# Two late steps for the first norm's halves and the second norm's routing in a fused attention and expert kernel

## Chip, cores and metric

One core of one Trainium2 chip. The metric is the device time of one execution in microseconds, median over runs; the kernel before has 318.69 us, median of 3 runs (318.09 to 318.78).

## What is computed

The input is 4 images of 128 channels and 32 x 32 positions, so 1024 tokens of 128 features each. Cut to what matters here:

```python
x = x + nin(softmax(q k^T / sqrt(128)) v)          # group norm, then one attention over 1024 positions
t = to_tokens(x)                                   # (4, 1024, 128)
u = ln(t)                                          # the first norm
k = softmax(u Wk, over tokens); ctx = k^T (u Wv)   # linear attention, 4 heads of 32
t = t + (u Wq) ctx Wout + b_out
w = ln(t)                                          # the second norm
probs = softmax(w router^T); top 2 of 8 experts, weights rescaled to sum 1
t = t + w + sum_e combine[:, e] * (gelu(w W1[e] + b1[e]) W2[e] + b2[e])
```

## The kernel before

The program is written out by hand for each engine: PE (matrix engine), ACT, DVE, POOL and the DMA queue SP. Each works through its own list in order and waits on semaphores. The first part handles the 4 images as batches: full attention of batch b, beside it the linear attention of batch b-1 and the routing of batch b-2. Then comes the **expert stage**, the subject here. It runs over 4 batches of 16 steps (2 halves of 512 tokens times 8 experts), 64 steps in all, numbered 0 to 63. In each step:

- PE: `hidden` forms the scores of one expert for one half of 512 tokens with `product3` (three matmuls of 512 columns, L1449 to L1451, from the high and low parts of `wT` and `w1`); it waits for the gelu of two steps earlier, since there are two score banks. Then `outward` forms the second product of the expert five steps earlier (`LAG` = 5) into the bank `ring`, with three matmuls again, or, for the steps in `WHOLE` (4, 6, 16, 18, 19, 20, 22, 28, 29, 30, 33, 34, 35, 37, 38, 40), with one in full float32 (L1805).
- ACT: `gelu` (L867, scores to `gel`), then `high` (L878), the high part of the weighed values of the step before; `WHOLE` steps have none.
- DVE: `weigh` (L1335, `gel` times the combine weights of that expert, which SP has spread over all partitions in one of four slots: `k_both`, `prob`, two halves of `pT_hi`), then `lower` (L1344, the low part of the step before). After five steps of a new half, `result` (L1356) adds the output bank, in PSUM, to the residual `z_in`.

The linear attention of the last batch and the routing of the last two are not done yet when the stage begins. They are put between the steps. `gathered` makes a table from step number to actions, and `between_steps` runs, on each engine, the actions of that number after that step's own work. The numbers stand in two tables, `TAIL_AT` (first half of the stage) and `END_AT` (last batch's routing). The units the prediction speaks of:

- `u0`, `u1`: PE turns (transposes, L1464) four 128x128 tiles of the first norm's result `u` each, and ACT copies them to `uT` (L741). POOL makes `u` in `first_norm` by eight instructions of 128x128 (`layer_norm`, L589), and signals after the fourth and the eighth. Its inputs are the mean and deviation that DVE hands it.
- `kT`: the keys (PE L1591 from `uT`), whose maximum DVE takes (`key_maximum`, L1112); ACT forms their exp, PE turns that back as `p0`, `p1`.
- `w0`, `w1`: the same for the second norm's result `w_n` (POOL L589): PE turns a half, ACT copies its high part (L745), DVE makes its low part (L1028).
- `lg`: the router's logits (PE L1640, L1641); ACT copies them (L765); `lT`: PE turns them (L1649). `rA`, `rB`, `rC`: DVE's top-2 and combine weights, some twenty short instructions from L1175 to L1212; `exp`: ACT's exponential for them (L771), with a table load before and after it. `z`: PE turns the residual that POOL made by `normed_residual` (L600), ACT copies it. `c`: PE turns the combine weights, DVE copies them (L1155), SP stores them and loads them back spread over the partitions (`load_shares`, L438).

The order of POOL's work is `w_n` of batch 2, `u` of batch 3 (`first_norm`), the residual L600 of batch 2, later `add_bout`, and then `w_n` and L600 of batch 3. The units' PSUM banks are dealt out in the order of the list `TAIL_UNITS` by `place_of`: the units after `OT1` take banks 0, 1 of `ring` and 2, 3 of `scores` in turn.

```python
def between_steps(steps, m, s):
    for step in steps.get(m * 2 * E + s, ()) if steps else ():
        step()
def turn_u(place, lb, n):
    pe.wait_ge(u_made, lb * HALVES + n + 1)
    turn(place, f"u{n}", tiles_of(u, n))
```

Of the kernel before, what the change touches and what calls it, by code (L numbers as in the profile page):

```python
# [47 lines left out]
LINEAR = dict(u=["u0", "u1"], kT=["kT0", "kT1"], p=["p0", "p1"])  # L48
ROUTING = dict(o=["o0", "o1"], w=["w0", "w1"], lg=["lg0", "lg1"], z=["z0", "z1"], c=["c0", "c1"])
# [9 lines left out]
                  OT1=1, v0=0, v1=1, T0a=2, T0b=3, T1a=0, T1b=1, xT0=2, xT1=3, w0=0, w1=1, T2a=2, T2b=3,  # L59
# [3 lines left out]

TAIL_FIRST = 2
TAIL_UNITS = (ATTENTION["T"][6] + ["ctx"] + ATTENTION["T"][7] + ["m2", "m3", "PV1"] + ROUTING["o"]
              + ["OT1"] + ROUTING["w"] + LINEAR["u"] + ROUTING["lg"] + ["lT"] + LINEAR["kT"]
              + ROUTING["z"] + LINEAR["p"] + ROUTING["c"] + ["g"])

END_UNITS = (["ctx", "m2", "m3"] + ROUTING["o"] + ROUTING["w"] + ROUTING["lg"] + ["lT"]
             + ROUTING["z"] + ROUTING["c"])  # L70


TAIL_AT = dict(m3=0, PV=1, o=2, st=2, OT=5, OTst=6, w0=9, w1=9, lg=12, u0=14, u1=14, lT=16, rA=17, kT=20, exp=20, rB=20, ks=23, z=21, p=21, rC=20, g=23, c=23)
END_AT = dict(ctx=24, m2=25, m3=27, o=29, st=29, w0=36, w1=36, lg=37, lT=38, rA=38, exp=38, rB=38, rC=38, z=41, c=41)

PIECES = 8
LAG, HELD, RING, PARTED = 5, 8, 6, 2
# [55 lines left out]
def conv_attention_moe(nc, x, gn_scale, gn_bias, wq, bq, wk, bk, wv, bv, wp, bp,  # L133
# [28 lines left out]
    with ctx:  # L162
# [145 lines left out]
        def gathered(*steps):  # L308

            found = {}  # L310
            for at, step in steps:
                found.setdefault(at, []).append(step)
            return found
# [370 lines left out]
        def _(act):  # L684
# [43 lines left out]
            def take_o(place, g):  # L728
                wait_filled(act, place, f"PV{g}")
                act.activation(o_s[:, :], ps(place, f"PV{g}"), ACT.Copy).then_inc(drained[place.bank(f"PV{g}")], 1)  # L730
# [8 lines left out]
            def turn_u(place, n):  # L739
                wait_filled(act, place, f"u{n}")  # L740
                act.activation(half(uT, n), ps(place, f"u{n}"), ACT.Copy).then_inc(drained[place.bank(f"u{n}")], 1)  # L741

            def turn_normed(place, kind, n, hi, made):
                wait_filled(act, place, f"{kind}{n}")
                act.activation(hi[n], ps(place, f"{kind}{n}"), ACT.Copy).then_inc(made, 1)  # L745

            def key_softmax(place, lb):

                act.wait_ge(k_max, lb + 1)
                for n in range(HALVES):  # L750
                    act.activation(half(p1, n), ps(place, f"kT{n}"), ACT.Exp, bias=kst[:, 2:3],
                                   accum_out=kst[:, 4 + n:5 + n]).then_inc(drained[place.bank(f"kT{n}")], 1)
# [8 lines left out]
            def take_logits(place):  # L761
                for n in range(HALVES):
                    unit = f"lg{n}"
                    wait_filled(act, place, unit)
                    act.activation(half(lgT, n), ps(place, unit)[0:2 * E, :], ACT.Copy  # L765
                                   ).then_inc(drained[place.bank(unit)], 1)

            def route_exp(place, lb):

                wait_drained(act, place, "lT")  # L770
                act.activation(rt[:, 1, :, :], rt[:, 0, :, :], ACT.Exp).then_inc(r_exp, 1)  # L771
# [9 lines left out]
            def w_halves(lb):  # L781
                return [wT_hi[:, bass.ds(lb * T + n * BANK, BANK)] for n in range(HALVES)]
# [97 lines left out]
            def experts(m, between):  # L880
# [10 lines left out]
            linear_and_routing = gathered(  # L891
                (TAIL_AT["PV"] + 3, lambda: take_o(TAIL, 1)),
                *((TAIL_AT["w" + str(n)], lambda n=n: turn_normed(TAIL, "w", n, w_halves(lc), w_hi_made)) for n in range(2)),
                *((TAIL_AT["u" + str(n)], lambda n=n: turn_u(TAIL, n)) for n in range(2)),
                (TAIL_AT["lg"], lambda: take_logits(TAIL)),
                (TAIL_AT["exp"], lambda: route_exp(TAIL, lc)),
                (TAIL_AT["exp"], lambda: key_softmax(TAIL, la)),
                (TAIL_AT["z"], lambda: turn_z(TAIL, lc, zT_late)),
                (TAIL_AT["p"], lambda: turn_keys(TAIL)),
                *((END_AT["w" + str(n)], lambda n=n: turn_normed(END, "w", n, w_halves(la), w_hi_made)) for n in range(2)),  # L900
                (END_AT["lg"], lambda: take_logits(END)),
                (END_AT["exp"], lambda: route_exp(END, la)),
                (END_AT["z"], lambda: turn_z(END, la, zT_late)),
            )
# [8 lines left out]
        def _(dve):  # L913
# [212 lines left out]
            def take_g(place):  # L1126
                take(place, "g", gT_s[:, :])
                wait_drained(dve, place, "g")
                dve.sem_inc(g_made, 1)
# [243 lines left out]
            def experts(m, between):  # L1373
# [37 lines left out]
                (TAIL_AT["g"], lambda: take_g(TAIL)),  # L1411
                (END_AT["ctx"], lambda: take_ctx(END)),
                (END_AT["m2"], lambda: take(END, "m2", m2T_s[:, :])),
                (END_AT["m3"], lambda: take(END, "m3", m3[:, :])),
# [472 lines left out]
```

## Time and profile before

| | before |
|---|---|
| median of 3 runs | 318.69 us (318.09 to 318.78) |
| profiled execution | span 315.6 us, first to last instruction (the page gives no other time for it) |
| PE busy | 297.7 us, 94% |
| DVE busy | 254.9 us, 81% |
| ACT busy | 200.8 us, 64% |
| POOL busy | 154.1 us, 49% |
| granted TensorE clock | 1.000 of full speed, mean |
| chain that ended last | PE 66%, DVE 13%, POOL 9%, ACT 7%, issue 3% |
| expert stage | from about 189 us on |

Busy time is the union of an engine's instructions. A matmul's end is modelled, so that the starts of matmuls, not their lengths, tell the pace of PE. The idle time of an engine is put down to what released it.

### The profile page before, as it was taken

The page shows a single profiled execution, that of the slowest core. Times are in us where ns is not written, and L with a number is a line of the kernel's source. Part 1 is how long each engine was busy: PE and PEld are TensorE (multiplying, and loading weights), DVE is VectorE, ACT ScalarE, POOL GpSimd, SP SyncE. Part 2 cuts the span into 40 slices and gives each one's busy share as a digit, 9 for nine tenths or more (in the row PEclk, how much of TensorE's full clock was granted, in tenths as well). Part 3 has the DMA queues.
Part 4 walks back from the last instruction along what each step waited for, and adds up shares of the span by engine and source line. Part 5 has one row for each costly group of instructions (what it writes and reads, how often), then busy time and mean ns, then how long its engine had stood idle before and what let it go on. Part 6 is the DMA issues. An engine that isn't in the chain of part 4 may idle for free.

```text
span 315.6 us, 5504 instructions
## 1 busy us (share of the span) xinstructions
PE 297.7 (94%) x1584; PEld 238.3 (76%) x1584; DVE 254.9 (81%) x635; ACT 200.8 (64%) x352; POOL 154.1 (49%) x358
## 2 busy tenths in 40 slices
PE   5898989989999999999999999998799998999996
PEld 4776768866878887878887797875677786668885
DVE  4599686587587799987698887999598896999996
ACT  3447474566771587663279577468578645888882
POOL 2899593059941985980784300599604049200000
PEclk9999999999999999999999999999999999999999
DMA  5902000010000021000000118395321783229801
GB/s 136 330 12 70 0 1 2 0 66 2 1 3 0 0 69 39 30 12 0 0 1 0 66 38 271 117 391 212 124 86 67 279 300 119 75 87 375 295 7 66
DMA packets 12904, 29.61 MB, mean 94 GB/s; under 512 B 2208, under 2 KB 6224, under 8 KB 10960
## 3 DMA queue, kind: packets, MB, share of 16 engines
q1 hardware_dynamic: 12448, 28.87, 26.3%
q10 hardware_dynamic: 432, 0.46, 0.4%
q8 instruction: 10, 0.16, 0.2%
q14 instruction: 14, 0.11, 0.1%
HBM read 24.73 MB, written 4.59 MB: 93 GB/s over the span
## 4 chain that ended last, share of the span: by engine, by line
PE 66%; DVE 13%; POOL 9%; ACT 7%; issue 3%; DMA 1%; DVEq 0%; POOLq 0%
PE ring L1464 11%; PE ring L1449 7%; PE ring L1451 7%; PE ring L1450 7%; PE scores L1449 6%; PE scores L1451 6%; PE scores L1450 6%; POOL w_n L589 3%; PE ring L1805 3%; POOL u L589 3%; ACT pT_hi L726 3%; ACT prob L720 2%; PE ring L1604 2%; DVE pT_lo L1059 2%; PE ring L1591 2%
## 5 line engine op out<-in xcount | busy, mean ns | idle before, releaser
L867 ACT ACTIVATE gel<-scores,b_c 128x512 f32<-128x512 f32 x64 | 43.9, 689 | 19.5 <-PE scores L1451 18.0
L1059 DVE TENSOR_TENSOR pT_lo<-ring,pT_hi 128x512 fp32r<-128x512 f32 x64 | 40.5, 681 | 9.8 <-ACT pT_hi L726 9.4
L720 ACT ACTIVATE prob<-prob,row_max 128x1024 f32<-128x1024 f32 x32 | 36.8, 1149 | 14.2 <-DVE prob L1052 14.2
L580 POOL TENSOR_SCALAR rstd<-lmv 128x4 f32<-128x4 f32 x16 | 4.3, 266 | 82.3 <-DVE lmv L1094 81.1
L1052 DVE TENSOR_SCALAR_CACHE_REDUCE prob<-scores 128x1024 f32<-128x1024 f32 x32 | 38.6, 1214 | 3.3 <-PE scores L1451 3.3
L726 ACT ACTIVATE pT_hi<-ring 128x512 fp32r<-128x512 f32 x64 | 34.6, 599 | 10.3 <-PE ring L1464 9.9
L1464 PE MATMUL ring<-ident,prob 128*128 128x128 f32 x256 | 33.7, 275 | 3.6 <-ACT prob L720 1.9
L1464 PEld LDWEIGHTS ring<-ident,prob 128*128 128x128 f32 x256 | 28.7, 140 | 8.5 <-ACT prob L720 3.7
L1449 PE MATMUL scores<-wT_hi,w_hi 128*128 128x512 f32 x64 | 29.3, 458 | 0.0
L1449 PE MATMUL scores<-k_both,q_hi 128*128 128x512 f32 x64 | 26.9, 421 | 1.9 <-DVE k_both L1037 1.3
L1449 PE MATMUL ring<-pT_hi,v_hi 128*128 128x512 f32 x64 | 26.5, 415 | 0.8 <-DVE pT_lo L1059 0.8
L1451 PE MATMUL scores<-k_both,q_lo 128*128 128x512 f32 x64 | 25.2, 393 | 0.0
L1451 PE MATMUL scores<-wT_hi,w_lo 128*128 128x512 f32 x64 | 25.1, 392 | 0.0
L1450 PE MATMUL scores<-wT_lo,w_hi 128*128 128x512 f32 x64 | 25.1, 392 | 0.0
L1450 PE MATMUL scores<-k_both,q_hi 128*128 128x512 f32 x64 | 25.1, 392 | 0.0
L1451 PE MATMUL ring<-pT_hi,v_lo 128*128 128x512 f32 x64 | 25.0, 391 | 0.0
L1450 PE MATMUL ring<-pT_lo,v_hi 128*128 128x512 f32 x64 | 25.0, 390 | 0.0
L611 POOL TENSOR_TENSOR t<-t,bout_row 128x128 f32<-128x128 f32 x32 | 14.0, 476 | 18.4 <-PE scores L1464 10.8
L730 ACT ACTIVATE o_s<-ring 128x512 f32<-128x512 f32 x8 | 4.8, 598 | 24.7 <-PE ring L1451 24.7
L589 POOL TENSOR_SCALAR u<-t,rstd 128x128 f32<-128x128 f32 x32 | 18.8, 608 | 0.9 <-POOL rstd L584 0.9
L589 POOL TENSOR_SCALAR w_n<-t,rstd 128x128 f32<-128x128 f32 x32 | 17.2, 555 | 0.9 <-POOL rstd L584 0.9
L584 POOL TENSOR_TENSOR rstd<-rstd,minus_half 128x4 f32<-128x4 f32 x16 | 16.6, 1040 | 0.0
(300 smaller groups left out, 780.9 us busy)
## 6 DMA issues: line engine op xcount, KB each, us to landing
pT_hi<-scratch_s SPq DMA_DIRECT2D x8, 1024.0 KB, 7.6
prob<-scratch_s SPq DMA_DIRECT2D x4, 1024.0 KB, 7.2
k_both<-scratch_s SPq DMA_DIRECT2D x3, 1024.0 KB, 5.8
z_in<-scratch_z SPq DMA_DIRECT2D x8, 256.0 KB, 2.9
out_dram<-out_s SPq DMA_DIRECT2D x7, 256.0 KB, 2.2
xb<-in_x_dram SPq DMA_DIRECT2D x3, 512.0 KB, 3.3
scratch_z<-out_s SPq DMA_DIRECT2D x2, 512.0 KB, 2.8
k_both<-scratch_s SPq DMA_DIRECT2D x4, 256.0 KB, 4.2
```

The lines of the kernel that those rows point to most:

```text
L584: pool.tensor_tensor(std[:, tiles], std[:, tiles], minus_half[:, tiles], ALU.pow).then_inc(ln_small[n], 1)
L589: last = pool.tensor_scalar(dst[:, j, :], src[:, j, :], neg[:, j:j + 1], std[:, j:j + 1], ALU.add, ALU.mult)
L611: last = pool.tensor_tensor(tiles_piece(t2, n), tiles_piece(t1, n), tiles_piece(bout_b, n), ALU.add)
L720: act.activation(prob[:, i % 2, :], prob[:, i % 2, :], ACT.Exp, bias=row_max[:, i:i + 1], scale=-1.0, accum_out=row_sum[:, 0, i:i + 1]).th ...
L726: act.activation(tile_group(pT_hi, n, i), as_tiles(ps(place, unit)), ACT.Copy).then_inc(p_hi_made, 1)
L867: act.activation(half(gel, s % 2), scores[:, s % 2, :], ACT.Gelu, bias=b1_c[:, s % E:s % E + 1]).then_inc(e_gelu, 1)
L1052: dve.tensor_scalar(prob[:, i % 2, :], scores[:, 2 * (i % 2):2 * (i % 2) + 2, :].rearrange("p a t -> p (a t)"), -SCALE, None, ALU.mult, AL ...
L1059: dve.tensor_tensor(tile_group(pT_lo, n, i), as_tiles(ps(place, unit)), tile_group(pT_hi, n, i).bitcast(FP32), ALU.subtract).then_inc(drai ...
L1449: pe.matmul(dst, lh, rh, start=start, stop=False)
L1450: pe.matmul(dst, lh, rl, start=False, stop=False)
L1451: return pe.matmul(dst, ll, rh, start=False, stop=stop)
L1464: last = pe.transpose(dst[0:t.shape[-1], j * step:j * step + rows], t, ident[0:rows, 0:rows])
```

## The change

Two tables of step numbers and one list change. In the expert stage, `u0` moves from step 14 to 15 and `u1` from 14 to 17, on PE and ACT. In the last batch's routing `w0` stays at step 36, and `w1` (PE, ACT and DVE), the logits, their turn, the whole of DVE's routing, ACT's exp, `z` and `c` each come one step later. The list `TAIL_UNITS` is put in the same order, by which the banks of `lg`, `u` and `lT` are dealt anew. No instruction is added or removed; POOL's and SP's order stays.

```diff
 TAIL_UNITS = (ATTENTION["T"][6] + ["ctx"] + ATTENTION["T"][7] + ["m2", "m3", "PV1"] + ROUTING["o"]
-              + ["OT1"] + ROUTING["w"] + LINEAR["u"] + ROUTING["lg"] + ["lT"] + LINEAR["kT"]
+              + ["OT1"] + ROUTING["w"] + ROUTING["lg"] + ["u0", "lT", "u1"] + LINEAR["kT"]
               + ROUTING["z"] + LINEAR["p"] + ROUTING["c"] + ["g"])
...
-TAIL_AT = dict(m3=0, PV=1, o=2, st=2, OT=5, OTst=6, w0=9, w1=9, lg=12, u0=14, u1=14, lT=16, rA=17, kT=20, exp=20, rB=20, ks=23, z=21, p=21, rC=20, g=23, c=23)
-END_AT = dict(ctx=24, m2=25, m3=27, o=29, st=29, w0=36, w1=36, lg=37, lT=38, rA=38, exp=38, rB=38, rC=38, z=41, c=41)
+TAIL_AT = dict(m3=0, PV=1, o=2, st=2, OT=5, OTst=6, w0=9, w1=9, lg=12, u0=15, u1=17, lT=16, rA=17, kT=20, exp=20, rB=20, ks=23, z=21, p=21, rC=20, g=23, c=23)
+END_AT = dict(ctx=24, m2=25, m3=27, o=29, st=29, w0=36, w1=37, lg=38, lT=39, rA=39, exp=39, rB=39, rC=39, z=42, c=42)
```

On ACT, from the gelu of step 14 on (L867 gelu, L878 high part, L741 copy of a half of `u`; `pT_lo` and `h_hi` hold high parts here). Before:

```order
L867 ACTIVATE gel<-scores,b_c 128x512
L878 ACTIVATE pT_lo<-hs 128x512
L741 ACTIVATE uT<-scores 128x512
L741 ACTIVATE uT<-ring 128x512
L867 ACTIVATE gel<-scores,b_c 128x512
L878 ACTIVATE pT_lo<-h_f 128x512
L867 ACTIVATE gel<-scores,b_c 128x512
L878 ACTIVATE pT_lo<-h_f 128x512
L867 ACTIVATE gel<-scores,b_c 128x512 x2
```

Now:

```order
L867 ACTIVATE gel<-scores,b_c 128x512
L878 ACTIVATE pT_lo<-hs 128x512
L867 ACTIVATE gel<-scores,b_c 128x512
L878 ACTIVATE pT_lo<-h_f 128x512
L741 ACTIVATE uT<-ring 128x512
L867 ACTIVATE gel<-scores,b_c 128x512
L878 ACTIVATE pT_lo<-h_f 128x512
L867 ACTIVATE gel<-scores,b_c 128x512
L741 ACTIVATE uT<-scores 128x512
L867 ACTIVATE gel<-scores,b_c 128x512
L878 ACTIVATE h_hi<-hw 128x512
```

Both copies of `u` stood between the high part of step 13 and the gelu of step 15; the first now stands behind the high part of step 14, the second behind the gelu of step 17.

On PE, behind the hidden product of step 14 (L1464 on `u` is a half's turn). Before:

```order
L1449 MATMUL ring<-h_hi,w_hi 128x512
L1450 MATMUL ring<-h_lo,w_hi 128x512
L1451 MATMUL ring<-h_hi,w_lo 128x512
L1464 MATMUL scores<-ident,u 128x128 x4
L1464 MATMUL ring<-ident,u 128x128 x4
L1449 MATMUL scores<-wT_hi,w_hi 128x512
L1450 MATMUL scores<-wT_lo,w_hi 128x512
L1451 MATMUL scores<-wT_hi,w_lo 128x512
L1449 MATMUL ring<-q_hi,w_hi 128x512
L1450 MATMUL ring<-q_lo,w_hi 128x512
L1451 MATMUL ring<-q_hi,w_lo 128x512
```

Now, from the outward product of step 15 on:

```order
L1449 MATMUL ring<-q_hi,w_hi 128x512
L1450 MATMUL ring<-q_lo,w_hi 128x512
L1451 MATMUL ring<-q_hi,w_lo 128x512
L1464 MATMUL ring<-ident,u 128x128 x4
L1449 MATMUL scores<-wT_hi,w_hi 128x512
L1450 MATMUL scores<-wT_lo,w_hi 128x512
L1451 MATMUL scores<-wT_hi,w_lo 128x512
L1449 MATMUL ring<-q_hi,w_hi 128x512
L1450 MATMUL ring<-q_lo,w_hi 128x512
L1451 MATMUL ring<-q_hi,w_lo 128x512
L1649 MATMUL scores<-ident,p 128x16 x8
```

The hidden and outward products of step 15 come before the first half's turn, and the second half's turn comes behind the logits' turn L1649 and step 17, below these rows.

On PE, in the last batch's routing, behind the outward product of step 31 (L1464 on `w_n` is the turn of `w0` and `w1`). Before:

```order
L1451 MATMUL ring<-pT_lo,w_lo 128x512
L1464 MATMUL scores<-ident,w_n 128x128 x8
L1449 MATMUL scores<-wT_hi,w_hi 128x512
L1450 MATMUL scores<-wT_lo,w_hi 128x512
L1451 MATMUL scores<-wT_hi,w_lo 128x512
L1449 MATMUL ring<-h_hi,w_hi 128x512
L1450 MATMUL ring<-h_lo,w_hi 128x512
L1451 MATMUL ring<-h_hi,w_lo 128x512
L1640 MATMUL ring<-wT_hi,router_two 128x512
L1641 MATMUL ring<-wT_lo,router_top 128x512
L1640 MATMUL ring<-wT_hi,router_two 128x512
```

Now:

```order
L1451 MATMUL ring<-pT_lo,w_lo 128x512
L1464 MATMUL scores<-ident,w_n 128x128 x4
L1449 MATMUL scores<-wT_hi,w_hi 128x512
L1450 MATMUL scores<-wT_lo,w_hi 128x512
L1451 MATMUL scores<-wT_hi,w_lo 128x512
L1449 MATMUL ring<-h_hi,w_hi 128x512
L1450 MATMUL ring<-h_lo,w_hi 128x512
L1451 MATMUL ring<-h_hi,w_lo 128x512
L1464 MATMUL scores<-ident,w_n 128x128 x4
L1449 MATMUL scores<-wT_hi,w_hi 128x512
L1450 MATMUL scores<-wT_lo,w_hi 128x512
L1451 MATMUL scores<-wT_hi,w_lo 128x512
```

Step 37's six products now stand between the two turns, and step 38's before the logits.

## Rows read from the trace of the kernel before

**Rows 1.** The page's first part: busy us, share of the span, instructions of each engine.

```profile
PE 297.7 (94%) x1584; PEld 238.3 (76%) x1584; DVE 254.9 (81%) x635; ACT 200.8 (64%) x352; POOL 154.1 (49%) x358
```

**Rows 2.** Waits of PE, 185 to 316 us: us in total, times, longest us.

```profile
PE ring L1464 <- POOL u L589: 2.1, 1, 2.1
PE scores L1464 <- POOL w_n L589: 1.0, 1, 1.0
```

**Rows 3.** Stretches: length; busy us (count) of PE, PEld, DVE, ACT, POOL; PEclk; DMA.

```profile
219.00:223.20 4.20, 1.34 (x10) 0.93 (x10) 2.54 (x5) 1.62 (x3) 4.20 (x7) 1.00 0.66 236
223.20:240.00 16.80, 16.80 (x82) 12.63 (x81) 14.18 (x36) 12.75 (x21) 5.96 (x14) 1.00 0.18 66
```

**Rows 4.** Timeline of PE: start us, length us, line, instruction, count [idle before, releaser].

```profile
218.79 0.39 PE L1451 MATMUL ring<-h_hi,w_lo 128*128 128x512 f32 x1
219.95 0.66 PE L1464 MATMUL scores<-ident,u 128*128 128x128 f32 x4 [0.77 <-POOL u L589]
222.69 0.66 PE L1464 MATMUL ring<-ident,u 128*128 128x128 f32 x4 [2.09 <-POOL u L589]
223.11 0.48 PE L1449 MATMUL scores<-wT_hi,w_hi 128*128 128x512 f32 x1
...
226.02 0.67 PE L1649 MATMUL scores<-ident,p 16*128 16x16 f32 x8
...
235.71 1.04 PE L1464 MATMUL scores<-ident,t 128*128 128x128 f32 x8
```

**Rows 5.** Timeline of POOL, whole passes and single tiles of them.

```profile
214.21 8.43 POOL L589 TENSOR_SCALAR u<-t,rstd 128x128 f32<-128x128 f32 x8 [0.22 <-POOL rstd L584]
...
215.67 1.91 POOL L589 TENSOR_SCALAR u<-t,rstd 128x128 f32<-128x128 f32 x1
...
219.88 0.44 POOL L589 TENSOR_SCALAR u<-t,rstd 128x128 f32<-128x128 f32 x1
...
220.31 1.47 POOL L589 TENSOR_SCALAR u<-t,rstd 128x128 f32<-128x128 f32 x1
...
222.61 3.38 POOL L600 TENSOR_TENSOR t<-t,w_n 128x128 f32<-128x128 f32 x8
...
266.36 4.29 POOL L600 TENSOR_TENSOR t<-t,w_n 128x128 f32<-128x128 f32 x8
```

**Rows 6.** Timeline of DVE, steps 13 to 20.

```profile
219.66 0.68 DVE L1356 TENSOR_TENSOR out_s<-ring,z_in 128x512 f32<-128x512 f32 x1
...
220.87 0.68 DVE L1344 TENSOR_TENSOR pT_lo<-hs,pT_lo 128x512 fp32r<-128x512 f32 x1
224.81 1.73 DVE L1335 TENSOR_TENSOR h_f<-gel,pT_hi 128x512 f32<-128x512 f32 x1 [3.27 <-ACT gel L867]
...
233.50 0.69 DVE L1112 TENSOR_REDUCE kst<-ring 128x1 f32<-128x512 f32 x1 [0.16 <-PE ring L1591]
```

**Rows 7.** Timeline of ACT, behind the last batch's routing exp.

```profile
273.87 1.27 ACT L867 ACTIVATE gel<-scores,b_c 128x512 f32<-128x512 f32 x2
```

**Rows 8.** Timeline of PE, the turns of `w0` and `w1` of the last batch.

```profile
264.71 0.60 PE L1464 MATMUL scores<-ident,w_n 128*128 128x128 f32 x4
266.33 0.66 PE L1464 MATMUL scores<-ident,w_n 128*128 128x128 f32 x4 [1.01 <-POOL w_n L589]
```

**Rows 9.** DVE in the last batch's routing, and L600 by itself (ns min/median/max).

```profile
268.44 1.01 DVE L1335 TENSOR_TENSOR hs<-gel,prob 128x512 f32<-128x512 f32 x1
...
271.46 0.29 DVE L1175 TENSOR_REDUCE logit<-scores 128x64 f32<-128x128 f32 x1
...
288.20 0.68 DVE L1335 TENSOR_TENSOR hs<-gel,k_both 128x512 f32<-128x512 f32 x1
...
L600 POOL TENSOR_TENSOR t<-t,w_n x32: 453/467/919, 108.6 to 269.7; 128x128 f32<-128x128 f32 x32
```

**Rows 10.** The last batch's first reload: issue (us), and us to landing.

```profile
283.07 0.33 SPq L438 DMA_DIRECT2D k_both<-scratch_s  x1
...
k_both<-scratch_s SPq DMA_DIRECT2D x1, 1024.0 KB, 4.7
```

## The prediction

> **What bounds the kernel now.** I read the page first: in a span of 315.6 us PE, the matrix engine, is busy for 94%, DVE for 81%, ACT for 64%, POOL for 49% [rows 1]. So PE sets the time wherever it doesn't stand still, and a move of work on PE pays only by ending an idle stretch. The list of waits, cut to PE in the expert stage, names what PE stands still for: the first norm's result `u` with 2.1 us in one wait, and `w_n` with 1.0 [rows 2]. The stretches agree: from 219.0 to 223.2 us PE works 1.34 of 4.20 us at a full clock, and is never idle in the 16.8 us behind [rows 3].
>
> Now each wait by itself, on PE's timeline. Step 14 ends with the product begun at 218.79; matmuls of this size follow each other by 0.23, so step 15 could begin at 219.02. Instead PE waits 0.77 for the first half of `u`, turns it, waits 2.09 for the second half, and begins step 15 at 223.11 [rows 4]. The source is POOL, whose eight tiles of `u` take 8.43 us from 214.21, to 222.64 [rows 5]. Single tiles show why: 1.47 or 1.91 us while DVE runs products of two operands in SBUF (as L1344 at 220.87), 0.44 while DVE takes one from PSUM (L1356 at 219.66) [rows 5, 6]. Behind PE, DVE stops too, 3.27 us until the next gelu [rows 6]. In the last batch's routing `w0` is turned at 264.71, and PE waits 1.01 for `w1`, which POOL hands over just before 266.33 [rows 8].
>
> The page gives its execution no time but the span of 315.6. The median of the runs is 318.69, 3.1 more; I carry the sum over as a difference.
>
> **The change, part by part.**
>
> *`u0` from step 14 to 15, `u1` from 14 to 17.* Nothing is added or removed: eight transposes and two ACT copies move. Two steps of two split products take 2.91 us (223.11 to 226.02), 1.46 each; a turn of four tiles whose input is there 0.42 (222.69 to 223.11), the logits' turn `lT` 0.6 [rows 4]. So step 15 begins at 219.02 and ends at 220.4; `u0`, there since 219.95, is turned with no wait. Step 16 runs from 220.85 to 222.3, `lT` to 222.9, step 17 to 224.35, and there PE asks for `u1`. POOL had it at 222.64, but its last two tiles were quick only because DVE stood idle from 221.55. That cover goes, since DVE gets its next gelu at once. With two quick tiles `u1` is ready at 222.6; with two of 1.47 behind 221.78, at 224.7; with three of 1.91 from 220.31, at 226.0 [rows 5]. The wait left lies between 0 and 1.7. I take 0.1, nearer the first two: DVE also pauses shortly for ACT, and a tile that meets a pause ends in it. Gain: 2.86 - 0.1 = **2.8 us**.
>
> *What is late next: the keys.* Steps 15 to 20 now run without the pause in which DVE and POOL drained. DVE works through from 224.81 to 233.34, 8.5 us, then waits 0.16 for the keys of step 20; the first of its products takes 1.73 us instead of 0.68, beside POOL's pass L600 of 222.61 [rows 5, 6]. Afterwards DVE starts this stretch at 221.47, right behind the L1344 of 220.87, and has it done at 230.0. The keys come 2.8 earlier than 233.50, at 230.7: 0.7 to spare. But L600 now lies under DVE's work in full. It may cost DVE no more than today, or its whole 3.4 us less the 1.05 of today, 2.3, which is 1.6 beyond the spare. The nearest row is L600 in the last batch, where DVE's product takes 1.01 instead of 0.68 [rows 5, 9]: five such products cost 1.7, 0.6 more than today, inside the spare. I put down **0.2** of loss.
>
> *L600 and `z`.* L600 must be done when PE turns `z`, at 235.71 now [rows 4], 232.9 then. It starts near 224.4. At 0.54 a tile (4.29 for eight, last batch) it ends at 228.7; at 0.92, its slowest tile, at 231.8; at 1.26, the mean of the first six tiles of `u` (214.21 to 221.78), at 234.5 [rows 5, 9]. I take the first two, no wait, because they are this operation's own; the third is a rival.
>
> [...] The rows show tiles of 1.47 and 1.91 us beside DVE products of 0.68 [rows 5, 6]. [...]
>
> *`w1` from step 36 to 37.* After `w0` (264.71 + 0.44) comes step 37, 1.46, so PE asks for `w1` at 266.6, after the 266.3 at which POOL hands it over [rows 8]. The wait of **1.0** goes whole.
>
> *Logits, `lT`, routing, `z` and `c` one step later.* PE's work stays the same. Counted from `w0`, DVE's routing chain begins one step later less the wait saved, 1.46 - 1.01 = 0.45 after the 271.46 of today [rows 9]. It now stands at step 39 in one piece. ACT loads tables before and after its exp, which needs that chain's start, and only then runs gelu 40: today at 273.87 [rows 7], then near 274.3, done at 275.0. PE needs it for step 42, which it reaches some 1.0 earlier than today, near 274.8. `z` then stands on ACT before gelu 43. These waits lie between 0 and the 1.0 won; I take **0.3**, since both meetings miss by 0.1 to 0.2.
>
> *The shares of the last batch.* The combine weights are copied a step later, so SP stores and reloads them later. Today the reload is issued at 283.07 and lands 4.7 us later, at 287.8; DVE's first product from it begins at 288.20: 0.4 spare [rows 9, 10]. Afterwards the copy comes some 0.9 later, the landing is at 288.7, and DVE, held by its own backlog, is there at 288.0: DVE waits 0.7. PE wants this product five steps later, 6.8 us, so the cost is 0, and stays so up to about one more microsecond.
>
> *SP's and POOL's queues* keep their order; the loads for other batches shift with the steps that free their slots.
>
> **Sum:** 318.69 - 2.86 - 1.01 + 0.1 + 0.2 + 0.3 = 315.4 us (span 312.3).
>
> **The rivals.**
>
> *A. Part comes back.* POOL's tiles run at 1.26 through L600 too. For it: six tiles of `u` in a row did. Against: DVE's routing instructions are short and let POOL in. L600 ends at 234.5, 1.6 after PE asks for `z`: 317.0. A key chain late by its full 1.6 gives the same.
>
> *B. Slower.* The same mechanism at the slowest tile seen, 1.91, wherever DVE has no pause: `u1` ready at 226.0 (1.6 beyond forecast), L600 done 15.3 later at 241.3, `z` asked for at 234.5, 6.8 waited. 315.4 + 8.4 = 323.8. It turns into a loss from about 1.5 us a tile of L600. For it: one of the eight tiles took it. Against: no tile of L600 took over 0.92 in this trace [rows 9].
>
> *C. No change.* DVE, not PE, is the bound from step 15 on, and PE's pause only moves to later steps. For it: the 8.5 us without a pause. Against: DVE is busy for 14.18 of the 16.8 us there [rows 3], and PE uses its products five steps behind. It gives 318.7.
>
> **How the numbers follow.** Forecast 0.74, A 0.15, C 0.06, B 0.05. Under 0.2% (0.64 us) a measurement can't tell a change; the three runs lie 0.69 apart. The floor is all 3.87 us of idle gone, 314.8, less 0.2 for that spread: 314.6. Above, the range takes in A with the same allowance: 317.2. Faster: forecast and A, 0.89; same 0.06; slower 0.05.
>
> **What would show it.** In the profile after, PE waits for `u` under 0.3 us and for `w_n` not at all; POOL's pass over `u` is longer than 8.43, by 0.5 to 2.5; DVE's pause of 3.27 is gone; the keys' first half reaches DVE near 230.7, and `w0` is turned near 262.1; the reload of `k_both` lands after DVE is ready for it, with no wait on PE. A wait of PE at `z` on L600 of over 0.5 us proves A or B right; many waits at L1449 for a gelu prove C. The sum is wrong if PE's idle behind 219 us isn't under 1 us in all.

## The result, and the profile after

The changed kernel takes 316.36 us, median of 12 runs (316.04 to 317.29); the kernel before, run beside it, 318.43 (12 runs, 317.08 to 320.60). The ratio is 0.9921, with a 95% interval of 0.9900 to 0.9942: faster, by some 2.1 us where 3.3 were forecast. The profiled executions differ by less: a span of 314.6 us against 315.6. In the profiles of three later kernels (e6, e8, e9 below) the granted clock was 0.50 for 3.4 us inside the stage; stretches outside that fall are read, and where one holds it (e8), the text says so. The ratios compare fast executions alone: one of e7's seven was slow, and without it its median is 316.45.

The page of the changed kernel, busy time and then the chain that ended last:

```profile
PE 298.5 (95%) x1584; PEld 238.4 (76%) x1584; DVE 255.1 (81%) x635; ACT 200.6 (64%) x352; POOL 156.8 (50%) x358
...
PE 74%; DVE 13%; ACT 7%; issue 4%; DMA 1%; DVEq 0%; ACTq 0%
```

PE works as much as before [rows 1]. POOL has left the chain, where it had 9%. POOL is busy 2.7 us longer with the same 358 instructions. Its waits, PE from 219 us to the end (us in total, times, longest):

```profile
PE scores L1449 <- ACT gel L867: 1.5, 2, 1.2
PE ring L1640 <- DVE wT_lo L1028: 0.7, 1, 0.7
```

The waits for `u` and `w_n` [rows 2] are gone, and three others stand in their place, 2.2 us together. None of them was there before. The stretch from 219 to 240 (columns as in [rows 3]) shows PE without a pause where it had stood still for 2.9 us:

```profile
219.00:240.00 21.00, 20.98 (x111) 15.83 (x110) 19.47 (x44) 16.30 (x28) 13.85 (x21) 1.00 0.35 125
```

The starts of the steps on PE (the first L1449 of each step's `hidden`, from the timelines of both kernels) tell where time was won and lost:

| step | before | after | ahead by |
|---|---|---|---|
| 15 | 223.11 | 219.15 | 3.96 |
| 16 | 224.57 | 220.87 | 3.70 |
| 18 | 228.11 | 225.14 | 2.97 |
| 36 | 262.68 | 259.81 | 2.87 |
| 39 | 271.35 | 267.55 | 3.80 |
| 45 | 282.12 | 279.46 | 2.66 |
| 51 | 290.52 | 287.96 | 2.56 |
| 52 | 291.88 | 290.69 | 1.19 |
| 63 | 307.35 | 306.29 | 1.06 |

(Steps 15, 18 and 39 don't have the same units ahead of them in both: behind 36 the turn `lT`, 0.6 us, stands before step 39 in the kernel before and behind it in the changed one. 36, 45 and the later ones compare directly.) The halves of `u` brought 2.9 us. From 36 to 45 the lead falls by 0.2: the 1.0 that `w1` wins is spent again by step 45, on a wait of 0.68 at the logits, one of 0.31 for a gelu, and small pieces. Then 1.4 are lost between 51 and 52.

Around the second loss, PE, then DVE and ACT, then SP in the changed kernel (timelines; start us, length us, and at the end the idle time before and what released it):

```profile
279.46 0.50 PE L1449 MATMUL scores<-wT_hi,w_hi 128*128 128x512 f32 x1 [0.31 <-ACT gel L867]
...
290.69 0.50 PE L1449 MATMUL scores<-wT_hi,w_hi 128*128 128x512 f32 x1 [1.20 <-ACT gel L867]
```

```profile
288.70 0.69 DVE L1335 TENSOR_TENSOR hs<-gel,k_both 128x512 f32<-128x512 f32 x1 [2.55 <-DMA k_both<-scratch_s]
```

```profile
289.43 0.63 ACT L878 ACTIVATE h_hi<-hs 128x512 fp32r<-128x512 f32 x1 [2.62 <-DVE hs L1335]
```

```profile
279.48 0.45 SPq L404 DMA_DIRECT2D scratch_s<-xT  x1
279.97 0.58 SPq L405 DMA_DIRECT2D scratch_c<-xT  x1
284.10 0.33 SPq L438 DMA_DIRECT2D k_both<-scratch_s  x1
```

DVE stands still for 2.55 us for the reload of the combine weights. ACT's `high` of step 48 waits 2.62 for that product of DVE, and it stands in ACT's list ahead of the gelu of step 50, which PE needs for its step 52: PE waits 1.20. The reload is issued 4.13 us after the store of `scratch_c`. Before, the store was issued at 280.91 and the reload at 283.07 [rows 10], 2.16 apart. That near doubling is the surprise of this case. DMA issues of the changed kernel from 275 to 300 us (KB each, us from issue to landing), then the two stores in the kernel before:

```profile
k_both<-scratch_s SPq DMA_DIRECT2D x1, 1024.0 KB, 4.5
...
scratch_c<-xT SPq DMA_DIRECT2D x1, 64.0 KB, 4.0
scratch_s<-xT SPq DMA_DIRECT2D x1, 32.0 KB, 2.3
```

```profile
scratch_c<-xT SPq DMA_DIRECT2D x1, 64.0 KB, 2.0
scratch_s<-xT SPq DMA_DIRECT2D x1, 32.0 KB, 2.3
```

(Both stores count on one semaphore here, so the 2.3 of `scratch_s` need not be its own landing; e6, with a semaphore for each, has 4.3.)

### The profile page after: what moved, and what is told of

Read it like the earlier page. It is cut to its first block, busy times and chain, and to the rows that moved or that the text cites. A ratio compares the mean times of both kernels' runs of the same rounds, so it can differ in the third digit from the quotient of the medians.

```text
span 314.6 us, 5504 instructions
## 1 busy us (share of the span) xinstructions
PE 298.5 (95%) x1584; PEld 238.4 (76%) x1584; DVE 255.1 (81%) x635; ACT 200.6 (64%) x352; POOL 156.8 (50%) x358
## 4 chain that ended last, share of the span: by engine, by line
PE 74%; DVE 13%; ACT 7%; issue 4%; DMA 1%; DVEq 0%; ACTq 0%
PE ring L1464 11%; PE ring L1449 8%; PE ring L1451 8%; PE ring L1450 8%; PE scores L1449 8%; PE scores L1451 7%; PE scores L1450 7%; PE ring L1805 3%; ACT pT_hi L726 3%; ACT prob L720 2%; PE ring L1604 2%; PE ring L1626 2%; DVE pT_lo L1059 2%; PE ring L1591 2%; DVE prob L1052 2%
## 5 line engine op out<-in xcount | busy, mean ns | idle before, releaser
L867 ACT ACTIVATE gel<-scores,b_c 128x512 f32<-128x512 f32 x64 | 43.7, 685 | 18.7 <-PE scores L1451 15.0
L1464 PE MATMUL ring<-ident,prob 128*128 128x128 f32 x256 | 33.7, 275 | 3.6 <-ACT prob L720 1.9
L1464 PEld LDWEIGHTS ring<-ident,prob 128*128 128x128 f32 x256 | 28.7, 140 | 8.5 <-ACT prob L720 3.7
L1449 PE MATMUL scores<-wT_hi,w_hi 128*128 128x512 f32 x64 | 30.1, 470 | 1.5 <-ACT gel L867 1.5
L1449 PE MATMUL scores<-k_both,q_hi 128*128 128x512 f32 x64 | 27.0, 421 | 1.6 <-DVE k_both L1037 0.9
L1449 PE MATMUL ring<-pT_hi,v_hi 128*128 128x512 f32 x64 | 26.6, 415 | 0.8 <-DVE pT_lo L1059 0.8
L589 POOL TENSOR_SCALAR u<-t,rstd 128x128 f32<-128x128 f32 x32 | 20.4, 655 | 0.9 <-POOL rstd L584 0.9
L1449 PEld LDWEIGHTS scores<-wT_hi,w_hi 128*128 128x128 f32 x64 | 12.1, 189 | 6.5 <-ACT gel L867 3.9
```

The source lines that it names most:

```text
L589: last = pool.tensor_scalar(dst[:, j, :], src[:, j, :], neg[:, j:j + 1], std[:, j:j + 1], ALU.add, ALU.mult)
L867: act.activation(half(gel, s % 2), scores[:, s % 2, :], ACT.Gelu, bias=b1_c[:, s % E:s % E + 1]).then_inc(e_gelu, 1)
L1449: pe.matmul(dst, lh, rh, start=start, stop=False)
L1464: last = pe.transpose(dst[0:t.shape[-1], j * step:j * step + rows], t, ident[0:rows, 0:rows])
```

## The experiments

The diffs show the main lines only. e1 to e4 ran in one set beside 23 runs of the kernel before (median 319.01), e5, e6, e7 and e10 in another, on another chip, beside 24 (319.01), e8, e9, e11 and e12 in a third beside 11 (319.27). Medians of different sets are compared by their ratios.

The **first part** below is the move of `u0` and `u1` with the list; the **second part** is the last batch's routing one step later. One number serves for all profiles: from the start of step 36 to that of step 63 on PE, 44.67 us before and 46.48 after. It holds the effects of the second part; e1, with the first part alone, has 44.67 as before.

**e1, the first part alone.**

```diff
-END_AT = dict(ctx=24, m2=25, m3=27, o=29, st=29, w0=36, w1=37, lg=38, lT=39, rA=39, exp=39, rB=39, rC=39, z=42, c=42)
+END_AT = dict(ctx=24, m2=25, m3=27, o=29, st=29, w0=36, w1=36, lg=37, lT=38, rA=38, exp=38, rB=38, rC=38, z=41, c=41)
```

> The change's first part alone: u0 at step 15, u1 at 17, the last routing as before. Theory 1 (the first part gives its whole wait back, the second part wins 1.0 us at w1 and loses more at the reload of the last shares): 2.9 us below the kernel before, span 312.8, faster than the whole change by 0.4 to 1.8 us; DVE waits under 0.3 us for the reload of k_both. Theory 2 (the first part leaves DVE behind, and that is paid at step 52): 2.0 us below at most, no faster than the whole change, and PE waits for a gelu at step 52 here too.

Measured: 315.46 us (6 runs, 314.86 to 315.69) beside 319.01 (23 runs), ratio 0.9905 [0.9876, 0.9933]; span 313.1. Steps 36 to 63 take 44.67, as before. PE's one wait behind 219 us, and SP:

```profile
PE scores L1464 <- POOL w_n L589: 1.0, 1, 1.0
```

```profile
278.41 0.59 SPq L405 DMA_DIRECT2D scratch_c<-xT  x1
280.56 0.33 SPq L438 DMA_DIRECT2D k_both<-scratch_s  x1
```

The wait of 1.0 stays, the store has its 2.15 us, DVE doesn't wait for the reload, and the span is 1.5 us shorter than with both parts. Expected were 2.9 us below the kernel before and a span of 312.8; it was 3.55 and 313.1.

**e2, the second part alone.** The tables the other way round: `TAIL_AT` and `TAIL_UNITS` as before, `END_AT` new. Against the change (`TAIL_UNITS` goes back too, not shown):

```diff
-TAIL_AT = dict(m3=0, PV=1, o=2, st=2, OT=5, OTst=6, w0=9, w1=9, lg=12, u0=15, u1=17, lT=16, rA=17, kT=20, exp=20, rB=20, ks=23, z=21, p=21, rC=20, g=23, c=23)
+TAIL_AT = dict(m3=0, PV=1, o=2, st=2, OT=5, OTst=6, w0=9, w1=9, lg=12, u0=14, u1=14, lT=16, rA=17, kT=20, exp=20, rB=20, ks=23, z=21, p=21, rC=20, g=23, c=23)
```

> The second part alone: w1, logits and routing of the last batch one step later, u as before. Theory 1: between no change and 0.8 us slower than the kernel before, with DVE waiting 1 to 3 us for the reload of k_both and PE over 0.5 us for the gelu of step 50. Theory 2: 1.0 us faster than before, and DVE waits for the reload under 1 us.

Measured: 320.43 us (12 runs), ratio 1.0061 [1.0037, 1.0085], slower by 1.4 us, more than the 0 to 0.8 expected; span 318.1, steps 36 to 63 46.71. Waits of PE:

```profile
PE ring L1464 <- POOL u L589: 2.4, 1, 2.4
PE scores L1449 <- ACT gel L867: 1.7, 2, 1.4
...
PE ring L1640 <- DVE wT_lo L1028: 0.7, 1, 0.7
```

The store is issued at 283.29 and the reload at 287.33, 4.04 later. So the losses belong to the second part, and it costs more than the 1.0 it wins: steps 36 to 63 are 2.0 us longer in all.

**e3, the shares before the residual.** In the change, two lines of SP's list swapped, which brings the stores of the shares ahead of a transfer of `z`.

```diff
-store_residual(END, B - 1, zT_late)
 store_shares(END, B - 1, cT_late)
+store_residual(END, B - 1, zT_late)
 load_shares(3, 0)
```

> The whole change, with the last batch's combine weights stored ahead of its residual in SP's queue. Theory 1: the reload is issued 0.6 to 2.5 us earlier (0.56 for the place in the queue, the rest if the store no longer meets the 16 KB instruction load of 281.7), DVE's wait for it shrinks from 2.55 to under 1.5 us, and the time is 0.4 to 1.3 us below the whole change. Theory 2: the same time as the whole change within 0.2 us.

Measured: 315.92 us (6 runs), ratio 0.9916 [0.9887, 0.9945]; span 314.1. SP and DVE:

```profile
280.04 0.59 SPq L405 DMA_DIRECT2D scratch_c<-xT  x1
280.80 0.38 SPq L397 DMA_DIRECT2D scratch_z<-xb  x1
283.24 0.33 SPq L438 DMA_DIRECT2D k_both<-scratch_s  x1
```

```profile
288.18 0.69 DVE L1335 TENSOR_TENSOR hs<-gel,k_both 128x512 f32<-128x512 f32 x1 [1.56 <-DMA k_both<-scratch_s]
```

Store to reload 3.20 instead of 4.13; DVE's wait falls by 1.0 and so does the stretch from 36 to 63, to 45.49. PE's waits for a gelu fall to 0.5.

**e4, the change again**, unaltered, in the set of e1 to e3.

> The changed kernel again, for the comparison on this chip and to see whether the late reload comes back. Both theories: 2.1 to 2.6 us below the kernel before. If the store of the weights meets the instruction load each time, it lands 3.5 to 4 us after its issue as in the first profile; if that was chance, 2 us after, and DVE waits under 1 us for the reload.

Measured: 317.45 us (12 runs, 316.23 to 319.15), ratio 0.9962 [0.9936, 0.9989]; span 314.4. Store to reload 4.06, DVE's wait 2.52, steps 36 to 63 46.49. The late landing is no chance of one execution. In this set e1's ratio lies below e4's, with intervals that do not meet.

**e5, the last reload in four quarters**, 256 KB each, so that the first product can go with the first quarter. DVE's products of the next three steps wait for their own.

```diff
-load_shares(3, 0)
+for e in range(QUAD):
+    sp.dma_start(half(share_slot[0], e), shares_of(B - 1, e, 1)).then_inc(share_first[e - 1] if e else share_loaded[0], 16)
```

> The whole change, with the last batch's first reload of k_both issued as four loads of 256 KB, one for each expert, in place of one of 1024 KB. If the landing of the reload is what the second part pays at step 52: the first quarter lands some 2.5 to 3 us after its issue instead of 4.5, DVE's wait of 2.5 us for it shrinks to about 1, PE's wait for the gelu at step 52 of 1.2 us goes, and the time is 1.0 to 1.3 us below the whole change. If the second part's loss lies elsewhere, the time stays within 0.3 us of the whole change.

Measured: 317.58 us (10 runs), ratio 0.9947 [0.9917, 0.9978]; span 314.8. DVE's wait 1.49, PE's at step 52 0.16, steps 36 to 63 45.56, 0.9 less than the change. Store to reload 4.17. The gain is in the profile; by the ratio e5 isn't told apart from the change in e4.

**e6, the reload behind a semaphore of its own.** It reads `scratch_s` alone; here it no longer waits for `scratch_c`, issued half a microsecond later.

```diff
+sp.dma_start(scratch_s[bass.ds(B - 1, 1)].rearrange("a r t -> (a r) t"), cT_late[0]).then_inc(shares_last, 16)
+sp.dma_start(scratch_c[bass.ds(B - 1, 1)].rearrange("a r t -> (a r) t"), cT_late[1]).then_inc(c_stored, 16)
+sp.wait_ge(shares_last, 16)
+sp.sem_inc(c_stored, 16)
```

> The whole change, with the reload of the last shares waiting only for the store it reads (scratch_s), not for scratch_c, whose last 12 packets come behind the 16 KB instruction load. If that meeting costs two microseconds: the reload is issued near 282.0 (some 2.3 us after the store's issue) instead of 284.0, DVE waits under 0.6 us for it, PE not at all at step 52, and the time is 1.0 to 1.4 us below the whole change. If the late reload came from the one step alone, the issue moves by under 0.5 us and the time stays.

Measured: 318.70 us (10 runs, 315.57 to 320.17), ratio 0.9976 [0.9940, 1.0012], not told apart from before. Missed: DVE still waits 2.21, steps 36 to 63 take 46.15, and the reload is issued 4.07 behind the second store. The DMA issues say why:

```profile
scratch_c<-xT SPq DMA_DIRECT2D x1, 64.0 KB, 4.0
scratch_s<-xT SPq DMA_DIRECT2D x1, 32.0 KB, 4.3
```

Both stores land late, so the wait is not an effect of which semaphore is asked. That sent me to the packets themselves, in the trace of the change. Between 281.25 and 283.25 (length us, clock, share of the DMA engines, GB/s), and what moved from 281.6 to 282.6, then from 282.6 to 283.4. A packet counts in the row in which it starts, so a long one that began at 281.71 is in the second row and not in the empty ones:

```profile
281.25:281.50 0.25, 1.00 0.90 258
281.50:281.75 0.25, 1.00 0.28 80
281.75:282.00 0.25, 1.00 0.00 0
...
282.50:282.75 0.25, 1.00 0.06 6
282.75:283.00 0.25, 1.00 0.09 10
283.00:283.25 0.25, 1.00 0.06 8
```

```profile
DMA packets 2, 0.02 MB, mean 17 GB/s; under 512 B 0, under 2 KB 1, under 8 KB 1
q8 instruction: 1, 0.02, 5.5%
```

```profile
DMA packets 13, 0.01 MB, mean 7 GB/s; under 512 B 2, under 2 KB 13, under 8 KB 13
q1 hardware_dynamic: 13, 0.01, 5.7%
```

The two stores have 192 packets of 512 bytes. 180 are done by 281.58. Then a single load of 16 KB on the queue "instruction" runs from 281.71 to 282.58, no other packet starts up to 282.5, and the last 12 packets, a sixteenth of all, run one after the other behind it, from 282.57 to 283.21. In the kernel before, all 192 are done at 282.51 and that load runs from 282.72. The other traces have it the same way. In all nine kernels with the second part the last 8 or 12 packets start only as such a load of 16 KB ends, or behind it (in e6, 12 of them up to 286.43; its load runs from 284.91 to 285.79). In all five without it the 192 packets are done 1.60 or 1.61 us after the issue of `scratch_c`, and the load comes later.

**e7, three edits at once**: the quarters of e5, the semaphore of e6, and on DVE the low part of `w1` directly behind `weigh` of step 37 (e10's edit).

> The whole change with the three edits together: quarters, own semaphore, early low part of w1. If the second part's loss is the wait at the logits (0.7), the gelu of step 45 (0.3) and the reload (1.2), then only some 0.3 of it is left and the wait of 1.0 for w1 is won: 3.5 to 3.9 us below the kernel before, 0.3 to 0.8 below the first part alone. If the meeting of routing and weighing on DVE costs by itself, it is no faster than the first part alone.

Measured: 316.50 us (7 runs), ratio 0.9910 [0.9874, 0.9946]; span 314.7. Missed: it reaches step 52 28.58 us behind step 36, 0.6 ahead of e1, but steps 36 to 63 take 45.52. DVE waits:

```profile
286.89 0.69 DVE L1350 TENSOR_TENSOR hs<-gel,k_both 128x512 f32<-128x512 f32 x1 [0.93 <-DMA k_both<-scratch_s]
...
291.44 0.69 DVE L1350 TENSOR_TENSOR h_f<-gel,k_both 128x512 f32<-128x512 f32 x1 [0.84 <-DMA k_both<-scratch_s]
...
293.89 0.69 DVE L1350 TENSOR_TENSOR hw<-gel,prob 128x512 f32<-128x512 f32 x1 [1.16 <-DMA prob<-scratch_s]
```

Later quarters and the next load, of `prob`, are now late, and PE waits 0.80 for a gelu at step 56. Four issues take SP 1.75 us (in e5's timeline) where one takes 0.33.

**e10, the low part early, alone** (on DVE, in the change):

```diff
 weigh(m, s)
+if m * 2 * E + s == END_AT["w1"]:
+    turn_normed(END, "w", 1, w_halves(wT_hi, la), w_halves(wT_lo, la), w_hi_made, la)
```

> The whole change, with DVE's low part of w1 put right behind the weighing of step 37, ahead of the lower of step 36 and of the result. The wait of PE for it at the logits (L1640 on wT_lo, 0.7 us) should go and DVE's routing begin 0.6 us earlier, so the reload too: 0.5 to 0.7 us below the whole change. If that wait is hidden by another behind it, no change within 0.2 us.

Measured: 316.19 us (4 runs), ratio 0.9898 [0.9846, 0.9949]; span 314.8. The logits no longer wait, and step 39 comes 0.95 sooner behind step 36 than in the change. The reload is issued 0.9 sooner too, but takes 4.8 us to land where it took 4.5, so that DVE's first product from it is only 0.54 sooner. That is what arrives at step 63: 45.93, 0.55 less. Waits of PE:

```profile
PE scores L1450 <- ACT gel L867: 1.9, 2, 1.6
```

DVE's wait for the reload has grown to 2.95, PE's at step 52 to 1.6.

**e12, the first part once more**, e1's kernel unaltered, beside e11.

> The first part alone, again, as the yardstick for the next one on the same chip: 2.9 to 3.5 us below the kernel before, 1.0 to 2.0 below what the whole change has shown, no wait of DVE for the reload of k_both.

Measured: 315.01 us (6 runs, 314.55 to 316.08) beside 319.27 (11 runs), ratio 0.9868 [0.9839, 0.9896]; span 313.1, steps 36 to 63 44.63. That is 4.3 us below the kernel beside it, more than the 2.9 to 3.5 expected.

**e11, the change with both losses taken away**: e10's edit, e3's swap, and the last reload as 256 KB and 768 KB.

```diff
-load_shares(3, 0)
+sp.dma_start(half(share_slot[0], 0), shares_of(B - 1, 0, 1)).then_inc(share_loaded[0], 16)
+sp.dma_start(share_slot[0][:, BANK:QUAD * BANK], shares_of(B - 1, 1, QUAD - 1)).then_inc(share_first[0], 16)
```

> The whole change with three edits: low part of w1 early, combine weights stored ahead of the residual, and the last reload split into the first expert's 256 KB and the other three's 768 KB. From step 36 to 63 the first part alone takes 44.7 us, the whole change 46.5. If logits, gelu and reload are all of the second part's loss, this takes 43.9 to 44.4 and is up to 0.8 us faster than the first part alone. If the routing in one piece at step 39 costs by itself, it stays above 44.7 and the first part alone is the better kernel.

Measured: 315.12 us (6 runs, 314.20 to 318.25), ratio 0.9889 [0.9850, 0.9927]; span 312.5, the shortest of all. Steps 36 to 63 take 44.16, 2.3 less than in the change and 0.5 less than before it. Left of the waits:

```profile
PE scores L1461 <- ACT gel L876: 0.3, 1, 0.3
```

```profile
286.27 0.69 DVE L1346 TENSOR_TENSOR hs<-gel,k_both 128x512 f32<-128x512 f32 x1 [0.99 <-DMA k_both<-scratch_s]
```

DVE waits 0.52 more for the 768 KB. So the second part's own idea is worth half a microsecond once its two side effects are gone. Swap and split weren't run without the second part; DVE has no wait there that they could end. The medians of e11 and e12 are not told apart.

**e8, `u1` at step 16 instead of 17**, on e1: how much room does the first part have?

```diff
-TAIL_AT = dict(m3=0, PV=1, o=2, st=2, OT=5, OTst=6, w0=9, w1=9, lg=12, u0=15, u1=17, lT=16, rA=17, kT=20, exp=20, rB=20, ks=23, z=21, p=21, rC=20, g=23, c=23)
+TAIL_AT = dict(m3=0, PV=1, o=2, st=2, OT=5, OTst=6, w0=9, w1=9, lg=12, u0=15, u1=16, lT=16, rA=17, kT=20, exp=20, rB=20, ks=23, z=21, p=21, rC=20, g=23, c=23)
```

> The first part alone with u1 at step 16, ahead of the logits' turn, in place of 17. PE gets there some 3.2 us after it begins step 15 (near 222.3 on the first profile's clock). If POOL is slowed for as long as DVE has no pause, u1 is ready only near 224.0 to 224.7, so PE waits 1.7 to 2.4 us for it and step 18 begins 1.5 us or more later than with 17. If POOL's last tiles stayed quick (222.6), PE waits 0.3 us.

Measured, one run: 319.07 us, span 317.3.

```profile
217.56 7.87 POOL L589 TENSOR_SCALAR u<-t,rstd 128x128 f32<-128x128 f32 x8 [0.22 <-POOL rstd L584]
```

```profile
PE scores L1464 <- POOL u L589: 1.6, 1, 1.6
```

PE waits 1.64 us for the second half. Behind that wait the granted clock falls: 1.00 up to 227 us, 0.56 from 227 to 229 and 0.72 from 229 to 232, means of the 0.50 that it has from 227.3 to 230.7 and the 1.00 on both sides of it, so the 8.41 us from step 15 to 18 (6.11 in e1, 5.71 in e12) hold both the wait and a slow piece. The wait is the reading: just under the 1.7 to 2.4 expected. Step 17 is needed.

**e9, fewer low parts on DVE**: steps 13, 14 and 15 also with one full-float32 product (`WHOLE`), on e1, so that DVE has fewer two-operand products beside POOL's pass.

```diff
-WHOLE = frozenset((4, 6, 16, 18, 19, 20, 22, 28, 29, 30, 33, 34, 35, 37, 38, 40))
+WHOLE = frozenset((4, 6, 13, 14, 15, 16, 18, 19, 20, 22, 28, 29, 30, 33, 34, 35, 37, 38, 40))
```

> The first part alone with steps 13, 14 and 15 whole, so DVE drops three products of two SBUF operands (and ACT three copies) while POOL makes u; the outward products of these steps are one float32 matmul each, 0.2 us longer, as for the other whole steps. If it is DVE's products that slow POOL, the pass over u takes 8.0 to 9.3 us in place of 10.0, with no single tile of 1.91 us behind step 13. If POOL is slow by itself here, it stays at 10.0.

Measured, one run: 318.99 us, span 317.3 (a wait of 2.6 for `w_n` at step 9, and a clock of 0.88 from 205 to 219 us).

```profile
216.78 6.96 POOL L589 TENSOR_SCALAR u<-t,rstd 128x128 f32<-128x128 f32 x8 [0.22 <-POOL rstd L584]
```

The eight tiles take 6.96 us, against 10.43 in e1, and none takes 1.91. That isn't shown to be the edit's doing. e12, which is e1's kernel with a wait of 0.8 at step 9, has 7.86, and e6, whose DVE has all its products here, had a wait of 2.1 there and takes less still:

```profile
215.94 5.68 POOL L597 TENSOR_SCALAR u<-t,rstd 128x128 f32<-128x128 f32 x8 [0.22 <-POOL rstd L592]
```

What settles the question is every tile of this pass in the 14 profiles, sorted by how many DVE products of two SBUF operands end while it runs:

| products ended | tiles | us of one tile |
|---|---|---|
| 0 | 42 | 0.44 to 0.45 |
| 1 | 12 | 0.70 to 0.97 |
| 2 | 25 | 0.96 to 1.49 |
| 3 | 33 | 1.65 to 1.99 |

So DVE's products do hold POOL up, as [rows 5, 6] had suggested, several in a row for one tile.

## Why the prediction was right or wrong

**`u0` and `u1`: right.** The forecast gain of 2.8 is there: to step 36 e1 needs 2.77 us less than before (70.94 against 73.71 from step 0) and the change 2.93. e12, e1's kernel again, needs 2.17 less: it is 1.1 behind the kernel before at step 13, with a wait of 0.82 for `w_n` at step 9 that the profiles of before and change don't have, and wins 3.3 from step 14 on. POOL in the changed kernel:

```profile
214.66 10.02 POOL L589 TENSOR_SCALAR u<-t,rstd 128x128 f32<-128x128 f32 x8 [0.22 <-POOL rstd L584]
224.64 4.30 POOL L600 TENSOR_TENSOR t<-t,w_n 128x128 f32<-128x128 f32 x8
```

The pass is 1.6 longer than [rows 5], within the 0.5 to 2.5 forecast: with DVE's pause of 3.27 gone, POOL lost its cover. Its tiles are 1.65, 1.91, 0.44, 1.39, 0.44, 1.91, 1.91, 0.44. (That holds for this profile; in e12, where DVE stood idle for 1.10 us early in the pass, it took 7.86.) Three of them take 1.91, as one tile of [rows 5] does, more than the 0.44 of a free tile and two products of 0.68 together. `u1` is ready at 224.67, between the bounds of 222.6 and 226.0 though not at the quick end that I took, and PE's asking at 224.5 met it: the wait is 0.2, for 0.1 put down. That the wait is so near is partly luck: POOL was 2.1 later than the end I took, and step 17 came just late enough (0.3 of wait in e1, none in e12, 1.6 in e8).

**Keys, L600 and `z`: right, a little too careful.** The keys' maximum stands at 230.62 (forecast 230.7) and nothing waits. L600 goes at 0.54 a tile, as in the last batch, and ends at 228.9. The 0.2 of loss put down didn't come; `w0` is turned at 261.85, 0.25 ahead of the forecast 262.1. Rivals A and B fall here. C falls as well: PE had no wait for a gelu up to step 44.

**`w1`: right.** PE turns it at 263.68 without a wait, and 1.0 is won:

```profile
261.85 0.60 PE L1464 MATMUL scores<-ident,w_n 128*128 128x128 f32 x4
263.68 0.60 PE L1464 MATMUL scores<-ident,w_n 128*128 128x128 f32 x4
265.27 0.79 PE L1640 MATMUL ring<-wT_hi,router_two 128*128 128x512 f32 x1
266.98 0.50 PE L1640 MATMUL ring<-wT_hi,router_two 128*128 128x512 f32 x1 [0.68 <-DVE wT_lo L1028]
```

**"PE's work stays the same", the logits: the step that was missed.** The last line above is a wait of 0.68 that I had not costed. In the unit's own step DVE has three instructions ahead of the low part of `w1`:

```profile
263.91 0.95 DVE L1335 TENSOR_TENSOR hs<-gel,prob 128x512 f32<-128x512 f32 x1
264.78 0.94 DVE L1344 TENSOR_TENSOR pT_lo<-hs,pT_lo 128x512 fp32r<-128x512 f32 x1
265.65 0.68 DVE L1356 TENSOR_TENSOR out_s<-ring,z_in 128x512 f32<-128x512 f32 x1
266.25 0.68 DVE L1028 TENSOR_TENSOR wT_lo<-scores,wT_hi 128x512 fp32r<-128x512 f32 x1
```

Two of them take 0.95 instead of 0.68, beside POOL's L600 (263.43 to 268.14). With `w1` at step 36, as in e1, DVE was idle for 0.98 before that low part. e10 shows it: with the low part moved ahead of step 37's `lower` and `result`, PE's wait goes.

It has a second consequence. DVE's routing chain starts 8.05 us behind `w0` (L1175 at 269.90) for 6.75 before, 1.30 later and not the 0.45 of the prediction. The step of 1.46 is there; the 1.01 in exchange is mostly used up by the 0.68 at the logits.

**The gelus: half right.** PE waits 0.31 for one, gelu 43 at step 45, where 0.3 was forecast for two meetings; gelu 40 isn't waited for.

**The shares: right that DVE waits, wrong in size and in the path to PE.** "DVE waits 0.7, so the cost is 0" was measured as 2.55 and 1.20. I had put the wait at 0.7 and said that one more microsecond would start to cost; 1.85 more came. (The prediction's 288.7 and 288.0 are on the clock of before, without the 2.6 that `w0` comes earlier; only their difference can be compared.) Two terms failed. The copy of the weights comes 1.9 us later counted from `w0` (store issued 18.12 behind it, before 16.20), and not 0.9, as the chain before it. And the time from the store's issue to the reload's was taken as fixed, where it grew by 1.97. Against these 3.0 us DVE itself was 1.0 later than forecast and the load landed 0.2 sooner. The time from store to reload:

| kernels | second part | store issue to reload issue, us |
|---|---|---|
| before, e1, e12, e8, e9 | no | 2.16, 2.15, 2.15, 2.16, 2.16 |
| change, e4, e2, e5, e6, e10 | yes | 4.13, 4.06, 4.04, 4.17, 4.07, 4.15 |
| e7, e11, e3 | yes, other orders or timing | 3.83, 3.66, 3.20 |

A load of 16 KB stands ahead of the last packets in all nine kernels with the second part and in none of the five without. Of the 1.97 us, 1.64 are that later last packet, 0.33 come behind it. That the load is the cause is argued from this order; no run moved the load by itself. What decides the meeting stays open: the load starts 1.74 us behind the store's issue in the change, 1.81 in the kernel before, and 1.87 in e5, where the 12 packets had not begun 0.26 us after the other 180 were done and the load had not started. What that load carries is not shown either.

The other error is the path. The ground for a cost of 0 was that PE wants the product five steps later, 6.8 us. ACT wants it first: its `high` stands ahead of the gelu that PE needs, and the room is 1.35 us. Nine profiles agree within 0.02 (us; DVE's wait for the first piece of the reload, and PE's at step 52):

| | e7 | e11 | e5 | e3 | e6 | e4 | change | e2 | e10 |
|---|---|---|---|---|---|---|---|---|---|
| DVE | 0.93 | 0.99 | 1.49 | 1.56 | 2.21 | 2.52 | 2.55 | 2.76 | 2.95 |
| PE | 0 | 0 | 0.16 | 0.20 | 0.86 | 1.17 | 1.20 | 1.41 | 1.61 |

**The sum.** By the starts on PE, steps 36 to 63 became 1.81 longer where the terms gave 0.7 shorter. The waits account for 1.18 of it: 0.68 + 0.31 + 1.20, less the 1.01 won. The other 0.6 lie in pieces of 0.1 to 0.25 between the same steps, and I haven't followed them. That the losses can be removed is shown by the same starts: early shares took 1.0 off (e3), the low part early 0.55 (e10), and both with the reload in two pieces 2.3 (e11).

**The median.** By the profiles the forecast is missed: a span of 312.3 was forecast and 314.6 came, and the condition set, PE idle under 1 us behind 219 us, failed with 2.2. That 316.36 lies inside the range is therefore luck, and the other executions show of what kind. The difference of 3.1 us between median and span, carried over from the kernel before, compares two different executions. In the 58 executions of that kernel whose span is on record, 1.68 to 2.21 us lie outside the span (1.69 in the profiled one of the change). So its profiled execution of 315.6 took 317.3 to 317.8, near the low end.

What most executions of the kernel before have more is a fall of the clock. In 42 of these 58 the mean granted clock is 0.987 to 0.995, median time 319.22; in the other 16 it is 1.000, median 318.02. The profiles of e6, e8 and e9 have a mean of 0.995, and each holds one stretch at 0.50 (in e8 from 227.3 to 230.7 us). None of the 24 executions of the change and none of the 12 with the first part alone is below 0.999. e2, which keeps the wait for `u`, has 6 of 12 at 0.994 or 0.995. So the medians gain something that no term of the sum had. That it was the wait for `u` that brought the falls is not shown: no trace of such an execution of the kernel before was kept, e6's fall comes behind a wait of 2.1 at step 9, and e6 has 4 of 10 executions at 0.995 though the wait for `u` is gone. The profiles say 1.1 us of gain, the medians 2.1, and the two ratios, 0.9921 and e4's 0.9962, 2.5 and 1.2.

**A kernel that beats both** is the first part alone: 0.9905 beside e4's 0.9962 in one set, with intervals that do not meet, and 1.8 us less from step 36 to 63 in each of its two profiles. Its second ratio is 0.9868; the change's first, 0.9921, has an interval that meets 0.9905's.

## What to carry to other kernels

Two moves that each end a wait are to be costed apart and tried apart; here one brought 2.8 us and the other took back more than it won. When a unit is moved by a step, ask on every engine that takes part in it what stands ahead of it in that step's own list, and follow the data to its last user, through stores and reloads; a wait that another engine hides is hidden only up to the slack, the slack is that of the nearest user (here ACT, with 1.35 us, and not PE with 6.8), and it is to be compared with the errors of all terms ahead of it together. A store, semaphore and reload in a row had no fixed price here: from issue to issue they took 2.15 us in one kernel and 4.17 in another. And before a difference between median and span is carried over, look whether the profiled execution is a typical one: its own time and clock beside those of the others say so.

## What was unexpected of the hardware

- The last 8 or 12 of 192 store packets came behind a load of 16 KB on the instruction queue, 0.88 us long in the change, in each of the nine kernels with the second part; `scratch_c` landed there after 4.0 us instead of 2.0 (the change against before).
- POOL's tiles of 128x128 took 0.44 us where none of DVE's products of two SBUF operands ended beside them, and up to 1.99 where three did in a row. POOL's L600, itself with two operands, took 0.54 a tile, while DVE's products grew from 0.68 to 0.95.
- In e8 the granted clock was 1.00 up to 227.3 us and 0.50 from there to 230.7; PE had been busy for 0.84 us of 223 to 225 and 1.52 of 225 to 227. In the kernel before, a wait of 2.09 us was followed by a clock of 1.00 [rows 3, 4]. The mean clock of the profiled execution was 0.995 in e6, e8 and e9, which hold such a stretch, and 0.998 to 1.000 in the other eleven, which have none outside their last 1.1 us.
